# A softmax denominator in cross-attention: three of four probability tiles added up by an accumulating transfer

## The chip, the cores and the metric

The kernel runs on one core of one Trainium2 chip. The metric is the device time of one execution, in microseconds (us). Five engines work in parallel, each through its own queue of instructions in program order: TensorE (PE in the profile; PEld is its weight load), VectorE (DVE), ScalarE (ACT), GpSimd (POOL) and SyncE (SP, which here only issues transfers). They meet through semaphores. Transfers run on the core's 16 DMA engines, whoever issues them. SBUF is the working memory of 128 partitions, PSUM the memory into which matmuls write.

## What is computed

The model is one layer: x (512 tokens of 512) attends to a context of 8192 rows of 384 (cross-attention, then an MLP), then to itself in a window (local attention), then comes a feed-forward block with quantised weights. Only the cross-attention is touched.

```python
def xattn(x, y, Wq, bq, Wk, bk, Wv, bv, W1, b1, W2, b2):     # x: 512 x 512, y: 8192 x 384
    q = (x @ Wq + bq).reshape(B, N, 16, 32)
    k = (y @ Wk + bk).reshape(B, M, 16, 32)
    v = (y @ Wv + bv).reshape(B, M, 16, 32)
    scores = jnp.einsum('bnhd,bmhd->bhnm', q, k) / sqrt(32)
    attn = jax.nn.softmax(scores, axis=-1)                    # over the 8192 keys
    out = jnp.einsum('bhnm,bmhd->bnhd', attn, v).reshape(B, N, 512)
    return jax.nn.relu(out @ W1 + b1) @ W2 + b2
```

The softmax needs, for each head and each of the 512 queries, the sum over all 8192 keys of exp(score). That sum, the denominator, is what the change is about.

## The kernel before

The cross-attention stage walks 16 heads. A head has 16 **quads** of 512 keys (`QUADS`), a quad has four **tiles** of 128 keys (`BT`). The names that matter:

- `scores` (L1079): for a tile, four fp16 matmuls side by side in the PE array write 128 keys x 512 queries to one of three PSUM banks. ACT (L1261) turns it into exp and writes it to `prob[:, q % 4, t]`, in SBUF, float32, 128 x 512. `prob` has four slots (`PSLOTS`), so quad q reuses the slot of quad q - 4.
- `pre` (L1042): the same product turned the other way round, for the head after the next one or so, from which DVE (L1297, `tile_max`) takes each query's maximum. Four tiles per quad. Its PSUM banks are three, too.
- `weighted` (L1092): for each quad, four float32 matmuls with the values, accumulated over the head in one bank.
- The denominator. Of a quad's four probability tiles, GpSimd adds the first `pool_tiles(q)` into `sum_pool` (L1435 and L1439): three tiles at q = 0, 1 and every odd q, two at the other even ones. `add_to_denominator` (L1103) puts the remaining one or two tiles through PE: products with a matrix of ones, which sum over the partitions, accumulated in the bank `den_ps`. Each such tile is four matmuls of 128 x 128, and is done two quads after its exp. At the head's end `denominator` (L1119) sends GpSimd's three summed tiles through the same products; it stands at the end of quad 1 of the next head. DVE then takes the reciprocal (`invert`, L1309) in quad 2, `output` (L1130) folds the weighted sums in quad 5, and DVE scales them (L1316) in quad 6.
- In the last head (15) GpSimd does nothing; DVE adds up two tiles of each quad (`sum_tiles`, L1345 and L1349) and PE takes the rest.

PE's order within a quad is written out by hand: `PE_ORDER = ((0,), 0, (1,), 1, "den", 2, (2,), 3, (3,))`, where `(j,)` is a `pre` tile, a number a `scores` tile and "den" the place of `add_to_denominator`; `weighted` of the quad before follows behind.

Before it writes a slot of `prob`, ACT waits until the slot's last readers are through: `pv_done` (the weighted product of quad q - 4), `den_added` (PE's ones-products of it) and `pool_summed` (GpSimd's add of it). GpSimd's own queue holds nothing but its adds in this stage. SP's queue issues the loads of keys (in four chunks per head, each 256 KB and 128 KB) and of values (1024 KB per head) for the head after the next, and the stores of the outputs.

Of the kernel before, what the change touches and what calls it, by code (L numbers as in the profile page):

```python
# [22 lines left out]
ALU = mybir.AluOpType  # L23
# [15 lines left out]
H = 16  # L39
# [19 lines left out]
POOL_TILES = 3  # L59
# [72 lines left out]
def perceiver(nc, a, out):  # L132

    with ExitStack() as whole:
# [104 lines left out]
        fold_in = sem("fold_in")  # L239
# [45 lines left out]
        with ExitStack() as st:  # L285
# [100 lines left out]
            def _(sp):  # L386
# [9 lines left out]
                sp.dma_start(fold[:], a["c_fold"]).then_inc(fold_in, 16)  # L396
# [453 lines left out]
        with ExitStack() as st:  # L850
# [12 lines left out]
            sum_pool = piece([2, POOL_TILES * T])  # L863
# [17 lines left out]
            pool_summed = sem("pool_summed")  # L881
            pv_read = sem("pv_read")
# [48 lines left out]
            def pool_tiles(q):  # L931

                return POOL_TILES if q < 2 or q % 2 else POOL_TILES - 1


            LAST_SUMMED = QUADS - 2

            def summed_tiles(h, q):

                if not (isinstance(h, int) and h == H - 1):  # L940
                    return pool_tiles(q)
                return DVE_TILES if q < LAST_SUMMED else 0
# [94 lines left out]
            def _(pe):  # L1037
# [58 lines left out]
                def add_to_denominator(i, s, q):  # L1096

                    h = 2 * i + s
                    if q == 0:
                        wait(pe, recip_ready, h)  # L1100
                    for n in range(summed_tiles(h, q), BT):
                        for t in range(TT):
                            last = nc.tensor.matmul(den_ps[t * HD:(t + 1) * HD, 0:P], ones[:],  # L1103
                                                    prob[:, q % PSLOTS, n, t * P:(t + 1) * P],
                                                    start=q == 0 and n == summed_tiles(h, q), stop=False)
                    last.then_inc(den_added, 1)

                def denominator(i, s):

                    h = 2 * i + s  # L1110
                    if isinstance(h, int) and h == H - 1:
                        pe.wait_ge(dve_summed, LAST_SUMMED)
                        tiles = DVE_TILES
                    else:
                        pe.wait_ge(pool_summed, QUADS * (h + 1))
                        tiles = POOL_TILES
                    for n in range(tiles):
                        for t in range(TT):
                            last = nc.tensor.matmul(den_ps[t * HD:(t + 1) * HD, 0:P], ones[:],  # L1119
                                                    sum_pool[:, s, n * T + t * P:n * T + (t + 1) * P],  # L1120
                                                    start=False, stop=n == tiles - 1)
# [17 lines left out]
                def head(i, s, first, last):  # L1139
# [3 lines left out]
                    for q in range(QUADS):  # L1143
                        ahead = last >= (1 if q < QUADS - AHEAD else 2)
                        for step in PE_ORDER:
                            if step == "den":
                                if q >= 2:
                                    add_to_denominator(i, s, q - 2)
                                elif not first:
                                    add_to_denominator(*before, QUADS - 2 + q)  # L1150
# [8 lines left out]
                        if q == 1 and not first:  # L1159
# [10 lines left out]
                pe.wait_ge(fold_in, 16)  # L1170
                pe.wait_ge(ones_row, 16)
# [12 lines left out]
                denominator(LASTPAIR, 1)  # L1184
# [43 lines left out]
            def _(act):  # L1228
# [64 lines left out]
            def _(dve):  # L1293
# [43 lines left out]
                def sum_tiles(q):  # L1337

                    sums = sum_pool[:, 1, 0:DVE_TILES * T].rearrange("p (n t) -> p n t", n=DVE_TILES)
                    if q:  # L1340
                        dve.wait_ge(p_ready, BT * quad_no(LASTPAIR, 1, q) + DVE_TILES)
                    if q == 1:

                        dve.wait_ge(den_ready, H - 2)
                        nc.vector.tensor_tensor(sums, prob[:, 0, 0:DVE_TILES], prob[:, 1, 0:DVE_TILES],  # L1345
                                                ALU.add).then_inc(dve_summed, 2)
                    elif q > 1:
                        dve.wait_ge(dve_summed, q)
                        nc.vector.tensor_tensor(sums, sums, prob[:, q % PSLOTS, 0:DVE_TILES],  # L1349
# [74 lines left out]
            def _(pool):  # L1424

                def add_up(i, s, q):
                    Q = quad_no(i, s, q)
                    n = pool_tiles(q)
# [877 lines left out]
```

## Time and profile before

| what | value |
|---|---|
| median of 3 runs | 1386.98 us |
| lowest and highest | 1385.68 and 1387.59 us |
| the profiled execution: span from first to last instruction | 1383.2 us |
| cross-attention stage, heads 0 to 14 | about 343 to 1079 us of the span |
| one head in that stage | about 48.6 us |

The profile is of one execution. Its span of 1383.2 us is 3.8 us short of the median of the runs; the profiled execution has no other time of its own. A row of a view by stretches gives for each engine the busy time in that stretch with the number of instructions in brackets, then the granted PE clock as a share of the full 2.4 GHz, the mean busy share of the 16 DMA engines, and what they moved.

### The profile page before, as it was taken

The page shows a single profiled execution, that of the slowest core. Times are in us where ns is not written, and L with a number is a line of the kernel's source. Part 1 is how long each engine was busy: PE and PEld are TensorE (multiplying, and loading weights), DVE is VectorE, ACT ScalarE, POOL GpSimd, SP SyncE. Part 2 cuts the span into 40 slices and gives each one's busy share as a digit, 9 for nine tenths or more (in the row PEclk, how much of TensorE's full clock was granted, in tenths as well). Part 3 has the DMA queues.
Part 4 walks back from the last instruction along what each step waited for, and adds up shares of the span by engine and source line. Part 5 has one row for each costly group of instructions (what it writes and reads, how often), then busy time and mean ns, then how long its engine had stood idle before and what let it go on. Part 6 is the DMA issues. An engine that isn't in the chain of part 4 may idle for free. (4 is left out here: it accounts for less than half of the span.)

```text
span 1383.2 us, 39979 instructions
## 1 busy us (share of the span) xinstructions
PE 1332.2 (96%) x17098; PEld 702.8 (51%) x17098; DVE 1120.9 (81%) x1786; ACT 806.1 (58%) x1459; POOL 778.7 (56%) x320
## 2 busy tenths in 40 slices
PE   7999999998999999999999999999999999999898
PEld 4444444443555555555555555545555445566454
DVE  5778888887888888888888888888887746578895
ACT  4454444443777777776777776776777841354332
POOL 0322222122899988988998898899889100201121
PEclk9999999999999999999999999999999999999999
DMA  8568777786352122122212112211210030491000
GB/s 265 177 169 231 207 211 211 210 238 177 91 183 69 39 69 67 30 65 67 69 39 68 56 38 69 67 50 57 59 66 31 5 145 1 92 214 41 0 9 23
DMA packets 127799, 137.54 MB, mean 99 GB/s; under 512 B 44995, under 2 KB 108995, under 8 KB 125699
## 3 DMA queue, kind: packets, MB, share of 16 engines
q1 hardware_dynamic: 127622, 134.98, 34.6%
q8 instruction: 135, 2.21, 0.7%
q14 instruction: 42, 0.34, 0.1%
HBM read 75.70 MB, written 44.17 MB: 87 GB/s over the span
## 5 line engine op out<-in xcount | busy, mean ns | idle before, releaser
L1297 DVE TENSOR_REDUCE early<-attend_banks 128x1 f32<-128x512 f32 x952 | 612.4, 685 | 80.8 <-PE attend_banks L1042 75.6
L1261 ACT ACTIVATE attend_prob<-attend_banks 128x512 f32<-128x512 f32 x1024 | 536.0, 599 | 200.8 <-PE attend_banks L1079 198.6
L1439 POOL TENSOR_TENSOR early<-early,attend_prob 128x1024 f32<-128x1024 f32 x210 | 614.5, 2926 | 37.7 <-ACT attend_prob L1261 9.6
L1079 PE MATMUL attend_banks<-early,k_first 97*32 97x512 f16 x2560 | 258.9, 382 | 3.1 <-ACT attend_prob L1261 3.1
L1042 PE MATMUL attend_banks<-k_first,early 96*32 96x512 f16 x2272 | 235.1, 382 | 1.1 <-PEq L285 1.1
L1079 PE MATMUL attend_banks<-early,attend_k_rest 97*32 97x512 f16 x1536 | 154.1, 381 | 2.8 <-ACT attend_prob L1261 2.8
L1042 PE MATMUL attend_banks<-attend_k_rest,early 96*32 96x512 f16 x1536 | 155.8, 380 | 0.0
L1103 PE MATMUL attend_banks<-attend_prob,ones 128*32 128x128 f32 x3048 | 134.3, 272 | 3.6 <-DVE attend_recip L1309 3.6
L1092 PE MATMUL attend_banks<-attend_prob,wkv_area 128*32 128x512 f32 x1024 | 134.1, 592 | 0.0
L1092 PE MATMUL attend_banks<-attend_prob,attend_vh_odd 128*32 128x512 f32 x1024 | 133.6, 592 | 0.0
L503 POOL TENSOR_TENSOR project_w_whole<-project_grid,project_qscale 128x704 f32<-128x704 f32 x24 | 33.3, 1386 | 173.0 <-DVE project_grid L636 173.0
L1103 PEld LDWEIGHTS attend_banks<-attend_prob,ones 128*32 128x32 f32 x3048 | 95.6, 110 | 54.5 <-DVE attend_recip L1309 11.1
L1079 PEld LDWEIGHTS attend_banks<-early,k_first 97*32 97x32 f16 x2560 | 77.3, 97 | 85.6 <-ACT attend_prob L1261 46.6
L1042 PEld LDWEIGHTS attend_banks<-k_first,early 96*32 96x32 f16 x2272 | 71.3, 97 | 58.4 <-issue 34.9
L555 ACT ACTIVATE project_v<-project_v_ps 128x512 f32<-128x512 f32 x64 | 38.1, 597 | 92.1 <-PE project_v_ps L771 92.1
L497 POOL TENSOR_TENSOR project_qn<-early,project_qinv 128x704 f32<-128x704 f32 x24 | 37.9, 1580 | 87.6 <-issue 50.2
L539 ACT ACTIVATE early<-project_k_ps,project_bk 128x512 f32<-128x512 f32 x64 | 44.0, 688 | 63.6 <-PE project_k_ps L752 61.6
L769 PE MATMUL project_v_ps<-project_w_hi,project_yT_hi 128*128 128x512 f16 x192 | 73.9, 385 | 5.7 <-ACT project_v L555 5.7
L1079 PEld LDWEIGHTS attend_banks<-early,attend_k_rest 97*32 97x32 f16 x1536 | 47.0, 96 | 57.8 <-ACT attend_prob L1261 38.1
L752 PE MATMUL project_k_ps<-project_yT_hi,project_w_hi 128*128 128x512 f16 x192 | 72.5, 379 | 2.3 <-ACT project_q_hi L574 1.4
L770 PE MATMUL project_v_ps<-project_w_lo,project_yT_hi 128*128 128x512 f16 x192 | 73.9, 385 | 0.0
L771 PE MATMUL project_v_ps<-project_w_hi,project_yT_lo 128*128 128x512 f16 x192 | 73.7, 384 | 0.0
(220 smaller groups left out, 1823.6 us busy)
## 6 DMA issues: line engine op xcount, KB each, us to landing
v_scratch<-project_v SPq DMA_DIRECT2D x16, 1024.0 KB, 8.9
early<-in_ctx_dram SPq DMA_DIRECT2D x16, 768.0 KB, 6.2
k_first<-k_scratch SPq DMA_DIRECT2D x36, 256.0 KB, 3.5
k_scratch<-project_k_hi SPq DMA_DIRECT2D x64, 128.0 KB, 2.9
k_scratch<-project_k_lo SPq DMA_DIRECT2D x64, 128.0 KB, 3.1
attend_vh_odd<-v_scratch SPq DMA_DIRECT2D x8, 1024.0 KB, 5.0
wkv_area<-v_scratch SPq DMA_DIRECT2D x7, 1024.0 KB, 4.8
attend_k_rest<-k_scratch SPq DMA_DIRECT2D x24, 256.0 KB, 3.5
```

The lines of the kernel that those rows point to most:

```text
L539: nc.scalar.activation(kf[:, g % 2], k_ps[:, g % 2], ACT.Identity, bias=bk[:, g:g + 1], scale=1.0 / WSCALE).then_inc(kf_ready, 1)
L752: last = nc.tensor.matmul(k_ps[:, g % 2], (w_lo if p == 2 else w_hi)[:, 0, k, cols], (yT_lo if p == 1 else yT_hi)[:, u, k], start=(k, p) = ...
L769: nc.tensor.matmul(v_ps[:, t % 2], yT_hi[:, u, k, cols], w_hi[:, 1, k], start=k == 0, stop=False)
L770: nc.tensor.matmul(v_ps[:, t % 2], yT_hi[:, u, k, cols], w_lo[:, 1, k], start=False, stop=False)
L771: last = nc.tensor.matmul(v_ps[:, t % 2], yT_lo[:, u, k, cols], w_hi[:, 1, k], start=False, stop=k == CK - 1)
L1042: last = nc.tensor.matmul(pre_ps[c * HD:(c + 1) * HD, bank, :], q_stack[0:KROWS, h, queries], keys_at(s, part * BLK, (part + 1) * BLK)[0:K ...
L1079: last = nc.tensor.matmul(s_ps[c * HD:(c + 1) * HD, s_bank[n], :], key_rows[:, c * HD:(c + 1) * HD], q_stack[0:KROWS + 1, h, :], start=Tru ...
L1092: last = nc.tensor.matmul(pv_ps[t * HD:(t + 1) * HD, :], vh[s][:, BT * q + t, :], prob[:, q % PSLOTS, t, :], start=q == 0, stop=q == QUADS ...
L1103: last = nc.tensor.matmul(den_ps[t * HD:(t + 1) * HD, 0:P], ones[:], prob[:, q % PSLOTS, n, t * P:(t + 1) * P], start=q == 0 and n == summ ...
L1261: nc.scalar.activation(prob[:, q % PSLOTS, t, :], s_ps[:, s_bank[BT * q + t]], ACT.Exp, scale=SCALE).then_inc(p_ready, 1)
L1297: nc.vector.tensor_reduce(part_max[:, s, j, part:part + 1], pre_ps[:, bank], AX.X, ALU.max).then_inc(pre_read, 1)
L1439: nc.gpsimd.tensor_tensor(sums, sums, prob[:, q % PSLOTS, 0:n], ALU.add).then_inc(pool_summed, 1)
```

## The change

GpSimd adds only one tile per quad (`POOL_TILES = 1`), the tile 0. The other three (`SENT_TILES`) are one contiguous piece of `prob` in each partition, 128 x 1536 float32 or 768 KB, and go by a transfer that GpSimd issues (`send`) into `sent[:, s, q % 2]`, which lies in SBUF, too. For q = 0 and 1 it is a plain copy, for the 14 others it has `accum_op=add`: the DMA engines read what is in the destination, add what they bring and write it back. There are two destinations, even and odd quads, each with its own semaphore `sent_in`. A send waits for the exps of its quad and for the send before it to the same destination.

PE has no more ones-products inside the heads 0 to 14. `denominator` takes seven tiles (one of GpSimd's, two times three of the transfers') in one block and stands at the end of quad 2 of the next head; `invert` moves from quad 2 to quad 4. ACT's wait before a slot is now for `pv_done`, `pool_summed` and `sent_in` of quad q - 4. In the last head the work is as before, but the products of quads 0 and 1 are made together in quad 3, since the denominator bank is taken until then. `sum_pool` shrinks and gets its own memory; the ones row's and the fold matrix's loads share a semaphore.

```diff
-POOL_TILES = 3
+POOL_TILES = 1
+SENT_TILES = BT - POOL_TILES
...
-            sum_pool = piece([2, POOL_TILES * T])
+            sent = piece([2, 2, SENT_TILES, T])
+            sum_pool = sb("sum_pool", [P, 2, POOL_TILES * T])
+            sum_last = sent[:, 1, 0, 0:DVE_TILES]
...
+            DEN_AT = 2
...
                 def denominator(i, s):
 
                     h = 2 * i + s
...
+                    wait(pe, recip_ready, h)
+                    pe.wait_ge(pool_summed, QUADS * (h + 1))
+                    tiles = [sum_pool[:, s, n * T:(n + 1) * T] for n in range(POOL_TILES)]
+                    tiles += [sent[:, s, u, n] for u in range(2) for n in range(SENT_TILES)]
+                    for n, tile in enumerate(tiles):
+                        if n == POOL_TILES:
+                            pe.wait_ge(sent_in[0], transfers(i, s, QUADS - 2))
+                            pe.wait_ge(sent_in[1], transfers(i, s, QUADS - 1))
+                        for t in range(TT):
+                            last = nc.tensor.matmul(den_ps[t * HD:(t + 1) * HD, 0:P], ones[:],
+                                                    tile[:, t * P:(t + 1) * P],
+                                                    start=n == 0, stop=n == len(tiles) - 1)
                     last.then_inc(den_ready, 1)
...
                             if step == "den":
-                                if q >= 2:
-                                    add_to_denominator(i, s, q - 2)
-                                elif not first:
-                                    add_to_denominator(*before, QUADS - 2 + q)
+                                if last == 0 and q > DEN_AT:
+                                    for behind in range(0 if q == DEN_AT + 1 else q - 2, q - 1):
+                                        add_to_denominator(i, s, behind)
...
-                        if q == 1 and not first:
+                        if q == DEN_AT and not first:
                             denominator(*before)
...
                         wait(act, pv_done, Q + 1 - PSLOTS)
-                        wait(act, den_added, Q + 1 - PSLOTS)
                         if last > 0 or q < PSLOTS:
                             wait(act, pool_summed, Q + 1 - PSLOTS)
+                            wait(act, sent_in[q % 2], transfers(i, s, q - PSLOTS))
                         else:
+                            act.wait_ge(den_added, q + 1 - PSLOTS)
...
-                        if q == 2 and not first:
+                        if q == (DEN_AT + 2 if last > 0 else DEN_AT) and not first:
                             invert(*before)
...
+                def send(i, s, q):
+                    pool.wait_ge(p_ready, BT * (quad_no(i, s, q) + 1))
+                    wait(pool, sent_in[q % 2], transfers(i, s, q - 2))
+                    if q < 2:
+                        wait(pool, den_ready, 2 * i + s - 1)
+                        nc.gpsimd.dma_start(sent[:, s, q % 2], prob[:, q % PSLOTS, POOL_TILES:BT]).then_inc(
+                            sent_in[q % 2], 16)
+                    else:
+                        nc.gpsimd.dma_start(sent[:, s, q % 2], prob[:, q % PSLOTS, POOL_TILES:BT],
+                                            accum_op=ALU.add).then_inc(sent_in[q % 2], 16)
+
+                def head(i, s):
+                    for q in range(QUADS):
+                        add_up(i, s, q)
+                        send(i, s, q)
```

PE's queue around the end of a head, before. L1042 is `pre`, L1079 `scores`, L1092 `weighted`, L1103 and L1119 the ones-products; the block of 12 is at the end of quad 1 of the next head.

```order
L1103 MATMUL attend_banks<-attend_prob,ones 32x128 x4
L1079 MATMUL attend_banks<-early,k_first 32x512 x4
L1042 MATMUL attend_banks<-k_first,early 32x512 x4
L1079 MATMUL attend_banks<-early,k_first 32x512 x4
L1042 MATMUL attend_banks<-k_first,early 32x512 x4
L1092 MATMUL attend_banks<-attend_prob,wkv_area 32x512 x4
L1119 MATMUL attend_banks<-early,ones 32x128 x12
L1042 MATMUL attend_banks<-attend_k_rest,early 32x512 x4
L1079 MATMUL attend_banks<-early,k_first 32x512 x4
L1042 MATMUL attend_banks<-attend_k_rest,early 32x512 x4
L1079 MATMUL attend_banks<-early,k_first 32x512 x4
L1103 MATMUL attend_banks<-attend_prob,ones 32x128 x4
```

The same engine after, at the end of quad 2 of the next head; each function's line is one or eleven higher (1043, 1080, 1093, 1130).

```order
L1080 MATMUL attend_banks<-early,k_first 32x512 x8
L1043 MATMUL attend_banks<-attend_k_rest,early 32x512 x4
L1080 MATMUL attend_banks<-early,k_first 32x512 x4
L1043 MATMUL attend_banks<-attend_k_rest,early 32x512 x4
L1093 MATMUL attend_banks<-attend_prob,wkv_area 32x512 x4
L1130 MATMUL attend_banks<-attend_sum_pool,ones 32x128 x4
L1130 MATMUL attend_banks<-early,ones 32x128 x24
L1043 MATMUL attend_banks<-attend_k_rest,early 32x512 x4
L1080 MATMUL attend_banks<-early,k_first 32x512 x4
L1043 MATMUL attend_banks<-attend_k_rest,early 32x512 x4
L1080 MATMUL attend_banks<-early,k_first 32x512 x8
```

The groups of four ones-products inside the quads are gone, so two `scores` tiles stand next to each other, and one block of 28 stands where 12 stood, a quad later.

GpSimd's queue in head 0 before, from its second quad:

```order
L1439 TENSOR_TENSOR early<-early,attend_prob 128x1024 [waits attend_pool_summed,attend_p_ready]
L1439 TENSOR_TENSOR early<-early,attend_prob 128x1536 [waits attend_pool_summed,attend_p_ready]
L1439 TENSOR_TENSOR early<-early,attend_prob 128x1024 [waits attend_pool_summed,attend_p_ready]
L1439 TENSOR_TENSOR early<-early,attend_prob 128x1536 [waits attend_pool_summed,attend_p_ready]
```

and after (L1455 and L1458 are the sends, copying and accumulating; `early` holds `sent`):

```order
L1455 DMA early<-attend_prob 128x1536 [waits attend_p_ready]
L1443 TENSOR_TENSOR attend_sum_pool<-attend_prob 128x512 [waits attend_p_ready]
L1455 DMA early<-attend_prob 128x1536 [waits attend_p_ready]
L1447 TENSOR_TENSOR attend_sum_pool<-attend_sum_pool,attend_prob 128x512 [waits attend_pool_summed,attend_p_ready]
L1458 DMA early<-attend_prob 128x1536 [waits attend_sent_in0,attend_p_ready]
L1447 TENSOR_TENSOR attend_sum_pool<-attend_sum_pool,attend_prob 128x512 [waits attend_pool_summed,attend_p_ready]
L1458 DMA early<-attend_prob 128x1536 [waits attend_sent_in1,attend_p_ready]
```

One add of two or three tiles per quad has become one add of one tile and one transfer of three, and each transfer waits in GpSimd's queue for the one two quads back.

## Rows read from the trace of the kernel before

**Rows 1.** The page: busy time, share of the span and instructions, by engine.

```profile
PE 1332.2 (96%) x17098; PEld 702.8 (51%) x17098; DVE 1120.9 (81%) x1786; ACT 806.1 (58%) x1459; POOL 778.7 (56%) x320
```

**Rows 2.** Busy time by stretches: start:end, length, engines, clock, DMA share, GB/s.

```profile
343.30:1079.00 735.70, 727.88 (x12908) 387.45 (x12908) 632.31 (x997) 523.02 (x998) 666.57 (x225) 1.00 0.22 64
398.00:446.50 48.50, 48.03 (x864) 25.78 (x858) 42.17 (x67) 34.60 (x66) 44.17 (x16) 1.00 0.46 143
645.00:693.00 48.00, 47.53 (x860) 25.84 (x853) 41.75 (x66) 34.41 (x66) 43.69 (x16) 1.00 0.20 59
336.00:350.00 14.00, 11.27 (x121) 6.33 (x123) 9.54 (x17) 7.02 (x12) 2.33 (x2) 0.88 0.89 261
```

**Rows 3.** Timeline of PE at a head's end: start, length, line, idle before.

```profile
493.56 1.04 PE L1092 MATMUL attend_banks<-attend_prob,attend_vh_odd 128*32 128x512 f32 x8
494.42 0.83 PE L1119 MATMUL attend_banks<-early,ones 128*32 128x128 f32 x24
495.08 0.40 PE L1042 MATMUL attend_banks<-k_first,early 96*32 96x512 f16 x4
495.30 0.40 PE L1079 MATMUL attend_banks<-early,k_first 97*32 97x512 f16 x4
...
496.34 0.43 PE L1103 MATMUL attend_banks<-attend_prob,ones 128*32 128x128 f32 x8 [0.21 <-DVE attend_recip L1309]
```

**Rows 4.** Groups of instructions, whole span: shapes and count, busy us, mean ns, idle.

```profile
L1103 PE MATMUL attend_banks<-attend_prob,ones 128*32 128x128 f32 x3048 | 134.3, 272 | 3.6 <-DVE attend_recip L1309 3.6
L1119 PE MATMUL attend_banks<-early,ones 128*32 128x128 f32 x376 | 13.1, 273 | 0.0
```

**Rows 5.** Waits of the stretch 400 to 1060 us: total us, times, longest.

```profile
ACT attend_prob L1261 <- PE attend_banks L1079: 176.5, 191, 1.4
DVE early L1297 <- PE attend_banks L1042: 66.6, 270, 0.5
PEld attend_banks L1079 <- ACT attend_prob L1261: 61.1, 215, 0.8
```

**Rows 6.** Groups by form, 400 to 1080 us: GpSimd's adds, DVE's work.

```profile
L1439 POOL TENSOR_TENSOR early<-early,attend_prob 128x1536 f32<-128x1536 f32 x98 | 340.5, 3475 | 21.7 <-ACT attend_prob L1261 9.6
L1439 POOL TENSOR_TENSOR early<-early,attend_prob 128x1024 f32<-128x1024 f32 x98 | 232.9, 2377 | 14.0
...
L1309 DVE RECIPROCAL attend_recip<-attend_banks 128x128 f32<-128x128 f32 x14 | 13.4, 957 | 9.0 <-PE attend_banks L1119 9.0
L1316 DVE TENSOR_TENSOR attend_o_out<-attend_banks,attend_recip 128x128 f32<-128x128 f32 x14 | 4.1, 292 | 4.7 <-issue 4.1 <-PE attend_banks L1130 0.6
L1304 DVE TENSOR_REDUCE early<-early 128x4 f16<-128x64 f32 x14 | 3.1, 220 | 0.5
```

**Rows 7.** Timelines: two of DVE's reductions on end, four of ACT's exps.

```profile
355.39 1.29 DVE L1297 TENSOR_REDUCE early<-attend_banks 128x1 f32<-128x512 f32 x2 [0.23 <-PE attend_banks L1042]
...
450.25 2.07 ACT L1261 ACTIVATE attend_prob<-attend_banks 128x512 f32<-128x512 f32 x4 [0.95 <-PE attend_banks L1079]
```

**Rows 8.** Busy time by stretches around a load of values issued at 735.86.

```profile
736.00:737.00 1.00, 1.00 (x30) 0.57 (x20) 0.94 (x2) 1.00 (x3) 0.12 (x1) 1.00 0.21 25
738.00:739.00 1.00, 1.00 (x28) 0.67 (x24) 0.67 (x2) 0.43 (x1) 0.93 (x1) 1.00 0.99 418
739.00:740.00 1.00, 1.00 (x28) 0.45 (x20) 0.64 (x1) 0.14 (x1) 1.00 (x1) 1.00 1.05 442
740.00:741.00 1.00, 0.79 (x20) 0.48 (x20) 1.00 (x3) 0.94 (x2) 1.00 (x1) 1.00 0.07 16
```

**Rows 9.** Transfers by issue: count, KB each, median us from issue to landing; SP's issue times.

```profile
attend_vh_odd<-v_scratch SPq DMA_DIRECT2D x8, 1024.0 KB, 5.0
local_kq_stack<-turned_area SPq DMA_DIRECT2D x24, 128.0 KB, 2.6
...
732.34 0.45 SPq L245 DMA_DIRECT2D attend_k_rest<-k_scratch  x1
732.84 1.82 SPq L246 DMA_DIRECT2D attend_k_rest<-k_scratch  x1
```

More of the change, by code:

```diff
@@ L881, in perceiver @@
             pool_summed = sem("pool_summed")
+            sent_in = [sem(f"sent_in{u}") for u in range(2)]
             pv_read = sem("pv_read")
@@ L929, in keys_at, with summed_tiles, transfers @@
                 return k_rest[:, lo - CHK:hi - CHK]
-            def pool_tiles(q):
-                return POOL_TILES if q < 2 or q % 2 else POOL_TILES - 1
             LAST_SUMMED = QUADS - 2
-            def summed_tiles(h, q):
-                if not (isinstance(h, int) and h == H - 1):
-                    return pool_tiles(q)
+            DEN_AT = 2
+            def summed_tiles(q):
                 return DVE_TILES if q < LAST_SUMMED else 0
+            def transfers(i, s, q):
+                return 16 * (quad_no(i, s, q) // 2 + 1)
             OUT_BANK = S_BANKS + turn_of["output"] % PRE_BANKS
@@ L1096, in add_to_denominator @@
                 def add_to_denominator(i, s, q):
-                    h = 2 * i + s
                     if q == 0:
-                        wait(pe, recip_ready, h)
-                    for n in range(summed_tiles(h, q), BT):
+                        pe.wait_ge(recip_ready, 2 * i + s)
+                    for n in range(summed_tiles(q), BT):
                         for t in range(TT):
@@ L1104, in add_to_denominator, with summed_last @@
                                                     prob[:, q % PSLOTS, n, t * P:(t + 1) * P],
-                                                    start=q == 0 and n == summed_tiles(h, q), stop=False)
+                                                    start=q == 0 and n == summed_tiles(q), stop=False)
                     last.then_inc(den_added, 1)
+                def summed_last():
+                    pe.wait_ge(dve_summed, LAST_SUMMED)
+                    for n in range(DVE_TILES):
+                        for t in range(TT):
+                            last = nc.tensor.matmul(den_ps[t * HD:(t + 1) * HD, 0:P], ones[:],
+                                                    sum_last[:, n, t * P:(t + 1) * P],
+                                                    start=False, stop=n == DVE_TILES - 1)
+                    last.then_inc(den_ready, 1)
                 def denominator(i, s):
                     h = 2 * i + s
[L1111 to L1117, printed above, removed]
+                    wait(pe, recip_ready, h)
[6 more added lines that the diff above has]
+                            pe.wait_ge(sent_in[1], transfers(i, s, QUADS - 1))
                         for t in range(TT):
                             last = nc.tensor.matmul(den_ps[t * HD:(t + 1) * HD, 0:P], ones[:],
-                                                    sum_pool[:, s, n * T + t * P:n * T + (t + 1) * P],
-                                                    start=False, stop=n == tiles - 1)
+                                                    tile[:, t * P:(t + 1) * P],
+                                                    start=n == 0, stop=n == len(tiles) - 1)
                     last.then_inc(den_ready, 1)
@@ L1168, in head @@
                             row(h + 1, 1 - s, n % PRE_BANKS)
-                pe.wait_ge(fold_in, 16)
-                pe.wait_ge(ones_row, 16)
+                pe.wait_ge(ones_row, 32)
                 pe.wait_ge(ones_set, 1)
@@ L1183, in _ @@
                 add_to_denominator(LASTPAIR, 1, QUADS - 1)
-                denominator(LASTPAIR, 1)
+                summed_last()
                 def hidden(m, chunks):
```

26 lines of the change are left out of this document (10 added, 16 removed).

## The prediction

> **What bounds the kernel now.** I read the busy shares first: PE is busy for 96% of the span, DVE 81%, the others under 60% [rows 1]. An average over stages says little of one stage, so the stretches come next. From 343.3 to 1079 us, heads 0 to 14, PE is busy for 727.9 of 735.7 us at the full clock; in one 48 us piece of it PE has 47.53, GpSimd 43.69, DVE 41.75, ACT 34.41, and the DMA engines are busy for a share of 0.20 [rows 2]. So PE sets the pace, 48.6 us per head or 3.04 us per quad. The waits agree: ACT and DVE wait for PE (176.5 and 66.6 us in 660); PE's matmuls wait for hardly anyone, only its weight loads do, ahead of time [rows 5]. DMA has four fifths of its time free, and nobody waits for it. That free time is what the change spends.
>
> **What one step of PE costs.** Busy times of matmuls overlap, so I take starts from the timeline [rows 3]. A group of four `pre` or `scores` matmuls starts 0.22 us before the next. The `weighted` group takes 494.42 - 493.56 = 0.86 us. The block of three ones-tiles takes 495.08 - 494.42 = 0.66, so 0.22 each. A quad without ones-products is 8 x 0.22 + 0.86 = 2.62 us.
>
> **What the change takes off PE.** Before, a head has 26 ones-tiles: 14 quads with one or two (7 x 2 + 7 x 1 = 21), quads 0 and 1 with one each, and 3 at the end. The trace bears it out: each tile leaves 8 records, 3048 / 8 = 381 = 15 x 23 + 36 and 376 / 8 = 47 = 15 x 3 + 2 [rows 4]. After, it has 7. So 19 tiles x 0.22 = 4.18 us per head go, 62.7 us for 15 heads. The stall of PE on the reciprocal, 3.6 us in all [rows 4], goes too, since the bank is next written a head later. Together 66 us. The last head has the same products, four tiles of them in one quad instead of two and two; I set that at nothing, as PE computes the same and waits for one reciprocal as before.
>
> **What hides the rest.** The block of seven tiles (1.54 us) stands behind a `weighted` group: 2.4 us without a new score. ACT has three banks to work through, at 2.07 / 4 = 0.52 us each, so it idles for about 0.9 us; it idles for 0.95 us in every quad now [rows 7], so it catches up. DVE's reductions start 1.29 - 0.69 = 0.60 us apart when nothing is missing (two of them in 1.29 us, of which the last has its 0.69) [rows 7]: 64 x 0.60 + 0.96 + 0.29 + 0.22 = 39.9 us per head [rows 6], under the 44.4 that PE would need. `invert` two quads later is still ahead of `output` in quad 5. GpSimd's add of one tile: two tiles take 2377 ns, three 3475, so one about 2377 - 1098 = 1.28 us [rows 6]. The issue of a transfer by GpSimd is not in the trace; SP's take 0.45 to 1.82 us [rows 9]. That makes 1.7 to 3.1 us per quad. I take the middle, 2.4, hidden under whatever the quad takes.
>
> **What the change adds: the DMA engines.** Fifteen heads send 16 pieces of 128 x 1536 x 4 = 786,432 bytes. First the plain price. In the middle of a load of values the engines are busy for a share of 0.99 and 1.05 and move 418 and 442 GB/s [rows 8]: at a full share 430 GB/s. A plain send is then 1.83 us of all 16 engines. That is the price of the two copies of each head, and the lower bound for an accumulating one; less than a copy it can't be, since it moves all that a copy moves. There is no accumulating transfer in this trace. What it has to do is plain, though: for each byte written two come in, that of the source and that of the destination. If the incoming side is as wide as a copy's, it takes 2 x 1.83 = **3.66 us**. If all three movements take turns, 3 x 1.83 = 5.49, my upper bound. I take 3.66: both reads are unavoidable and 430 GB/s is a busy share of 1.0, so I see no room for the second read; the write can go beside them as in a copy.
>
> The transfers that are there already stay: a share of 0.22 of 735.7 us = 162 us of all engines [rows 2]. The sum for heads 0 to 14:
>
> 15 x (2 x 1.83 + 14 x 3.66) + 162 = 15 x 54.9 + 162 = 985.5 us of DMA time, where the stage had 735.7 us and PE would now want 735.7 - 66 = 669.7.
>
> The engines are then the bound, and the stage is 985.5 - 735.7 = 250 us longer: 1383.2 + 250 = **1633 us** of span, and with the 3.8 us by which the runs' median lies above the span **1637 us**, against 1387.
>
> **Who waits.** A late transfer holds up GpSimd (the send two quads later, and the add queued behind it), and through `sent_in` ACT, which can't write the slot of quad q - 4; then PE has no exps for `weighted` and no free score bank, and the `pre` tiles that DVE wants are queued behind. Nothing is left to cover it; everyone runs at DMA's pace, 64.6 us per head or about 4.1 per quad. The chain of each destination could be tighter still: landing of a 128 KB move within SBUF takes 2.6 us [rows 9], of which 0.3 are data, so an accumulating send about 2.3 + 3.66 + 1 for its issue = 7 us, and there are two chains: 3.5 us per quad, just under DMA's own 3.66. So I add nothing for it.
>
> A rule of the Trainium skill bears on this price. "Collectives: The Full Stack", section "The bandwidth ceiling", holds that a reducing transfer is slower than a copying one not for the addition but for its two source reads on one ring, with a measured ratio of 1.93. As an estimate from that page an accumulating send would be 1.93 x 1.83 = 3.53 us and the result 1609 us. No run here shows it yet.
>
> **The rivals.**
>
> *Rival 1, not slower: the second read is free.* If the engines read faster than they write, an accumulating send costs what a copy does. DMA then needs 15 x 16 x 1.83 + 162 = 601 us, less than PE's 669.7; PE stays the bound and the kernel gains the whole 66: **1321 us**. It decides at a price: up to (669.7 - 162 - 15 x 3.66) / 210 = 2.16 us per send the gain is whole, and at 2.47 us, where the same sum is made with 735.7, it is nil. For it speaks that the 430 GB/s may be set by memory outside SBUF or by the write; against it that both directions would have to be far from equal.
>
> *Rival 2, in between: the price lies between 2.3 and 3.2 us.* At 2.8 us the stage takes 15 x (3.66 + 39.2) + 162 = 805 us, the kernel about **1456 us**. The same place is reached if GpSimd is late: its add and an issue of 1.82 us make 3.1 us per quad, 49.6 per head, 15 us over the 15 heads, **1402 us**; that needs a cheap transfer as well.
>
> *Rival 3, worse: more than a doubled copy.* At 5.49 us the stage takes 15 x (3.66 + 76.9) + 162 = 1370 us and the kernel **2021 us**. Halfway there, another way leads through the clock. PE would be busy for about 670 of 985 us, and in the one stretch of this trace that is as idle, 336 to 350 us with 11.27 of 14 busy, the granted clock is 0.88 [rows 2]. At 1.2 GHz a quad would take 5.5 us of PE, more than DMA's 4.1; if that held half the time, 240 x 0.5 x 1.4 = 168 us come on top: about **1805 us**.
>
> *Rival 4, that it does not do what it says.* The order of instructions shows that the ones-products are gone and 16 sends per head are there, so this has no chance of its own.
>
> **How the numbers follow.** DMA-bound at a price near 3.66 (3.3 to 4.3 us, 1560 to 1770 us): 0.63. Rival 1: 0.15. Rival 2: 0.12. Rival 3: 0.10. The predicted time is that of the first, 1637. The range runs from 1400 to 1850: it leaves out rival 1 (0.15) and about half of rival 3 (0.05). A change of 0.2% (3 us) is about what a measurement here can tell from none. Faster: rival 1 and a sliver of rival 2, 0.16. Same: the narrow window around a price of 2.47 us, 0.02. Slower: the rest, 0.82.
>
> **What the profile after would show.** In the same heads: DMA share near 1.0 where 0.20 stood; PE busy 65 to 70% of the stretch, ACT waiting for a DMA and no longer for PE; 64 to 65 us per head; sends landing 6 to 9 us after their issue; GpSimd busy for a third. I am wrong if the DMA share stays below 0.9 while the head takes over 48.6 us (then the chain, the issue or the add sets the pace, not the engines' capacity), or if heads take 44 us with PE at 99% (rival 1). If PE's granted clock is below 1.00 there, part of the loss is the clock's.

## The result, and the profile after

The changed kernel takes 1702.5 us (median of 4 runs, 1699.9 to 1703.6) against 1386.6 us before: a ratio of 1.2275, with a 95% interval of 1.2258 to 1.2293. It is slower by 316 us. The forecast was 1637 us, with a range of 1400 to 1850. The profiled execution has a span of 1701.8 us, 318.6 us more than the profiled one before.

The page's busy times, to be set beside [rows 1]:

```profile
PE 1387.4 (82%) x14818; PEld 616.3 (36%) x14818; DVE 1116.3 (66%) x1786; ACT 804.5 (47%) x1459; POOL 608.3 (36%) x560
q0 software_dynamic: 34560, 188.76, 53.3%
q1 hardware_dynamic: 127622, 134.98, 27.9%
```

PE has 2280 records fewer, which is the ones-products (285 tiles of 8). The second and third line are from the list of DMA queues: packets, MB, and the time of their packets as a share of 16 engines' span. q0 is new; it holds the sends, 240 x 786,432 bytes = 188.7 MB.

The stage by stretches, columns as in [rows 2] (start:end, length, PE, PEld, DVE, ACT, POOL, granted clock, DMA share, GB/s):

```profile
343.30:1400.00 1056.70, 786.05 (x10696) 302.59 (x10700) 630.74 (x1000) 524.35 (x1005) 496.86 (x465) 0.90 1.00 223
650.00:700.00 50.00, 36.07 (x512) 13.14 (x507) 32.06 (x53) 26.51 (x51) 25.05 (x23) 0.97 1.04 211
```

The DMA share, 0.20 to 0.22 before, is 1.00 over a thousand microseconds. No compute engine is over 75% busy. Who waits for whom has turned round against [rows 5] (total us, times, longest; here over the whole span):

```profile
PEld attend_banks L1080 <- ACT attend_prob L1271: 434.3, 422, 5.5
DVE early L1307 <- PE attend_banks L1043: 398.0, 377, 6.6
POOL early L1458 <- DMA early<-attend_prob: 369.3, 171, 5.2
ACT attend_prob L1271 <- DMA early<-attend_prob: 356.5, 148, 6.3
PE attend_banks L1080 <- ACT attend_prob L1271: 260.8, 163, 5.0
```

This is the chain of the forecast: a send waits for the send two quads back, ACT for its slot, PE for the exps, DVE for PE. The sends themselves, in GpSimd's timeline (start, length, line, idle before):

```profile
742.66 0.89 POOL L1458 DMA_DIRECT2D early<-attend_prob  x1 [1.53 <-DMA early<-attend_prob]
746.39 0.89 POOL L1458 DMA_DIRECT2D early<-attend_prob  x1 [1.55 <-DMA early<-attend_prob]
751.12 0.89 POOL L1458 DMA_DIRECT2D early<-attend_prob  x1 [2.52 <-DMA early<-attend_prob]
755.31 0.89 POOL L1458 DMA_DIRECT2D early<-attend_prob  x1 [1.99 <-DMA early<-attend_prob]
759.00 0.89 POOL L1458 DMA_DIRECT2D early<-attend_prob  x1 [1.50 <-DMA early<-attend_prob]
762.74 0.89 POOL L1458 DMA_DIRECT2D early<-attend_prob  x1 [1.54 <-DMA early<-attend_prob]
```

Three of the five distances are 3.69 to 3.74 us. The two behind the load of keys issued at 744.50 are 4.73 and 4.19. The stretch of the shortest one, with no load issued in it:

```profile
755.31:759.00 3.69, 3.01 (x44) 1.23 (x44) 2.15 (x4) 2.65 (x6) 2.19 (x2) 1.00 1.04 211
```

The engines are full, and one send of 768 KB goes through in that time. So an accumulating send costs the 16 engines about 3.7 us when it has them to itself. A head takes 69.6 us, from the first reciprocal to the one 13 heads later:

```profile
431.87 0.95 DVE L1319 RECIPROCAL attend_recip<-attend_banks 128x128 f32<-128x128 f32 x1
...
1336.31 0.95 DVE L1319 RECIPROCAL attend_recip<-attend_banks 128x128 f32<-128x128 f32 x1
```

Landing has become slow for everyone. Against the 5.0 us of [rows 9] a load of values takes 10.9:

```profile
early<-attend_prob POOLq DMA_DIRECT2D x240, 768.0 KB, 7.9
attend_vh_odd<-v_scratch SPq DMA_DIRECT2D x8, 1024.0 KB, 10.9
```

The changed kernel was run again beside the experiments:

> The changed kernel again, beside the others on the same chip: 1702 us.

It gave 1703.3 us, a ratio of 1.2286 (1.2261 to 1.2310). Ratios in this document are against the kernel before, run beside each experiment (1385.7 to 1386.6 us), with the 95% interval in brackets.

### The profile page after: what moved, and what is told of

It is laid out like the page before. It is cut to its first block and busy times, and to the rows that moved or that the text cites. A ratio compares the mean times of both kernels' runs of the same rounds, so it can differ in the third digit from the quotient of the medians.

```text
span 1701.8 us, 35926 instructions
## 1 busy us (share of the span) xinstructions
PE 1387.4 (82%) x14818; PEld 616.3 (36%) x14818; DVE 1116.3 (66%) x1786; ACT 804.5 (47%) x1459; POOL 608.3 (36%) x560
## 3 DMA queue, kind: packets, MB, share of 16 engines
q1 hardware_dynamic: 127622, 134.98, 27.9%
## 5 line engine op out<-in xcount | busy, mean ns | idle before, releaser
L1080 PE MATMUL attend_banks<-early,k_first 97*32 97x512 f16 x2560 | 241.3, 406 | 179.0 <-ACT attend_prob L1271 179.0
L1458 POOL DMA_DIRECT2D early<-attend_prob x210 | 186.0, 886 | 410.9 <-DMA early<-attend_prob 369.3
L1447 POOL TENSOR_TENSOR attend_sum_pool<-attend_sum_pool,attend_prob 128x512 f32<-128x512 f32 x210 | 324.9, 1547 | 4.0 <-ACT attend_prob L1271 3.1
L1043 PE MATMUL attend_banks<-k_first,early 96*32 96x512 f16 x2272 | 246.9, 411 | 1.1 <-PEq L285 1.1
L1080 PE MATMUL attend_banks<-early,attend_k_rest 97*32 97x512 f16 x1536 | 143.9, 405 | 81.8 <-ACT attend_prob L1271 81.8
L1043 PE MATMUL attend_banks<-attend_k_rest,early 96*32 96x512 f16 x1536 | 160.2, 405 | 0.0
L1093 PE MATMUL attend_banks<-attend_prob,attend_vh_odd 128*32 128x512 f32 x1024 | 148.7, 659 | 0.0
L1093 PE MATMUL attend_banks<-attend_prob,wkv_area 128*32 128x512 f32 x1024 | 148.3, 658 | 0.0
L752 PE MATMUL project_k_ps<-project_yT_lo,project_w_hi 128*128 128x512 f16 x192 | 72.4, 379 | 0.2 <-DVE project_yT_lo L599 0.2
L752 PE MATMUL project_k_ps<-project_yT_hi,project_w_lo 128*128 128x512 f16 x192 | 72.4, 379 | 0.0
## 6 DMA issues: line engine op xcount, KB each, us to landing
attend_vh_odd<-v_scratch SPq DMA_DIRECT2D x8, 1024.0 KB, 10.9
```

The costliest lines, as they stand in the source:

```text
L752: last = nc.tensor.matmul(k_ps[:, g % 2], (w_lo if p == 2 else w_hi)[:, 0, k, cols], (yT_lo if p == 1 else yT_hi)[:, u, k], start=(k, p) = ...
L1043: last = nc.tensor.matmul(pre_ps[c * HD:(c + 1) * HD, bank, :], q_stack[0:KROWS, h, queries], keys_at(s, part * BLK, (part + 1) * BLK)[0:K ...
L1080: last = nc.tensor.matmul(s_ps[c * HD:(c + 1) * HD, s_bank[n], :], key_rows[:, c * HD:(c + 1) * HD], q_stack[0:KROWS + 1, h, :], start=Tru ...
L1093: last = nc.tensor.matmul(pv_ps[t * HD:(t + 1) * HD, :], vh[s][:, BT * q + t, :], prob[:, q % PSLOTS, t, :], start=q == 0, stop=q == QUADS ...
L1447: nc.gpsimd.tensor_tensor(sums, sums, prob[:, q % PSLOTS, 0:POOL_TILES], ALU.add).then_inc(pool_summed, 1)
L1458: nc.gpsimd.dma_start(sent[:, s, q % 2], prob[:, q % PSLOTS, POOL_TILES:BT], accum_op=ALU.add).then_inc(sent_in[q % 2], 16)
```

## Experiments

**The addition left out (copy3).** The question was whether the second read makes the price, or anything sent by GpSimd is slow.

```diff
-                        nc.gpsimd.dma_start(sent[:, s, q % 2], prob[:, q % PSLOTS, POOL_TILES:BT],
-                                            accum_op=ALU.add).then_inc(sent_in[q % 2], 16)
+                        nc.gpsimd.dma_start(sent[:, s, q % 2], prob[:, q % PSLOTS, POOL_TILES:BT]).then_inc(sent_in[q % 2], 16)
```

> The changed kernel with all 16 sends of a head as plain copies; the sums of the sent tiles are left out, so the denominators are those of two quads only. In the changed kernel, where no load is under way, the sends follow each other every 3.73 us. Theory A (the accumulating send reads source and destination, twice the incoming bytes, and the 16 DMA engines are full): a copy costs 1.83 us, heads 0 to 14 need 15 x 16 x 1.83 + 162 = 601 us of DMA, less than PE's 670, so PE is the bound again: about 1321 us, 44.4 us per head, DMA share about 0.9. Rival B (a transfer issued by GpSimd is slow whatever it does, by its descriptors or its issue): no change, about 1690 us. Rival C (the chain: a send waits for the landing two quads back): a landing falls by 1.9 us to about 6, so 3.0 us per quad, about 1390 us.

Measured: 1435.4 us, ratio 1.0356 (1.0326 to 1.0387). Taking the addition out gives back 267 of 317 us. That settles most of it against rival B. But 1321 did not come either. The queue's row, the stretch 500 to 1000 us and three waits in it:

```profile
q0 software_dynamic: 34560, 188.76, 35.2%
500.00:1000.00 500.00, 454.10 (x6825) 187.32 (x6817) 395.15 (x643) 329.59 (x634) 272.37 (x300) 0.97 0.84 297
ACT attend_prob L1271 <- DMA early<-attend_prob: 36.4, 16, 7.8
PE attend_banks L1130 <- DMA early<-attend_prob: 25.2, 10, 3.8
PE attend_banks L1080 <- ACT attend_prob L1271: 20.5, 30, 2.6
```

35.2% of 1432.5 us over 240 copies is 2.10 us each. With 2.10 the forecast's sum for DMA is 15 x 16 x 2.10 + 162 = 666 us, level with the 670 that it gave PE, and the stage takes some 785 us (735.7 and the 49.3 by which the span is longer). The row agrees that the engines are not full on average (0.84). Yet PE is idle for a tenth of the time. The timelines of PE, GpSimd and SP at one head's end show how:

```profile
505.84 0.57 POOL L1458 DMA_DIRECT2D early<-attend_prob  x1 [0.16 <-issue]
506.16 0.34 SPq L965 DMA_DIRECT2D wkv_area<-v_scratch  x1
509.58 0.53 POOL L1455 DMA_DIRECT2D early<-attend_prob  x1 [3.17 <-ACT attend_prob L1271]
511.31 0.39 PE L1130 MATMUL attend_banks<-attend_sum_pool,ones 128*32 128x128 f32 x8
514.96 2.39 PE L1130 MATMUL attend_banks<-early,ones 128*32 128x128 f32 x48 [3.25 <-DMA early<-attend_prob]
```

The head's last send leaves at 505.84, the load of values (1024 KB) at 506.16, and the next send at 509.58. The engines carry all three at once, and PE's block of ones-products stands idle for 3.25 us, until the last sends have landed. The DMA share of this stretch, near 1 for nine microseconds:

```profile
506.00:515.00 9.00, 5.75 (x96) 2.17 (x91) 5.12 (x9) 4.65 (x10) 2.23 (x3) 1.00 0.97 370
```

An average share of 0.84 hides moments in which it is near 1.0 and somebody waits.

**The block moved back (copy3_den3).** If PE's wait at the block were the cost, moving it would bring it back. The edit comes on top of copy3's; the last head keeps its block where it was.

```diff
-            DEN_AT = 2
+            DEN_AT = 3
```

> The run with plain copies (1435 us) with the block of seven ones-tiles one quad later, at the end of quad 3 (quad 2 of the last head), and the reciprocal at quad 5; sums of the sent tiles left out as there. That run's PE waits at the block for the last sends of the head before, 25.2 us in 500 (10 heads). If this wait is what a late landing costs PE, about 2.5 us per head go: 1435 - 38 = about 1397 us. If the sends only meet the next wait (ACT's, for its slot), it stays at 1425 to 1435 us.

Measured: 1437.2 us, ratio 1.0372 (1.0351 to 1.0393), no gain. The waits of the stretch 500 to 1000 us:

```profile
ACT attend_prob L1271 <- DMA early<-attend_prob: 59.4, 33, 4.3
POOL early L1458 <- DMA early<-attend_prob: 101.3, 54, 4.1
PE attend_banks L1080 <- ACT attend_prob L1271: 42.8, 48, 3.6
```

PE's wait at the block is gone from the longest ones, ACT's wait for its slot has grown from 36.4 to 59.4 us, and PE's for ACT from 20.5 to 42.8, nearly what the block had given back. So the block was only the first to meet the late landings. The expectation that 38 us would come back was wrong. That they are late because of the loads beside them is my reading of the timeline above; no run moved a load or gave `prob` more slots.

**No sends (nosend).** What PE's part of the change is worth by itself. The block takes GpSimd's one sum seven times in place of the sent tiles.

```diff
-                        if n == POOL_TILES:
-                            pe.wait_ge(sent_in[0], transfers(i, s, QUADS - 2))
-                            pe.wait_ge(sent_in[1], transfers(i, s, QUADS - 1))
...
-                            wait(act, sent_in[q % 2], transfers(i, s, q - PSLOTS))
...
-                        send(i, s, q)
```

> The changed kernel without any send and without the waits on them; the block of seven ones-tiles stays, and takes GpSimd's one sum seven times, so tiles 1 to 3 of each quad are left out of the denominator. It measures what PE's part of the change is worth alone. Forecast of the blind sum: 66 us less than before, 1321 us; 44.4 us per head. If DVE or ACT or the block of seven sets the pace instead, it stays over 1335 us.

Measured: 1342.4 us, ratio 0.9686 (0.9658 to 0.9714): 43 us less than before, not 66. A head takes 45.8 us (reciprocals at 447.08 and 492.87). PE's timeline has the reason:

```profile
587.72 0.61 PE L1080 MATMUL attend_banks<-early,attend_k_rest 97*32 97x512 f16 x8
588.16 0.39 PE L1043 MATMUL attend_banks<-k_first,early 96*32 96x512 f16 x4
588.46 0.40 PE L1080 MATMUL attend_banks<-early,attend_k_rest 97*32 97x512 f16 x4
588.68 0.39 PE L1043 MATMUL attend_banks<-k_first,early 96*32 96x512 f16 x4
588.90 1.03 PE L1093 MATMUL attend_banks<-attend_prob,attend_vh_odd 128*32 128x512 f32 x8
```

Without the ones-products two `scores` tiles stand next to each other (the x8). PE is then ahead of ACT by a tile, and the fourth `scores` starts 0.30 instead of 0.22 us after the group before it, in this quad and in those around it. If it is so in all, 16 x 0.08 = 1.3 us per head is 19 us in 15 heads. The next run tests this.

**PE's order made alternating (nosend_alt, before_alt).**

```diff
-PE_ORDER = ((0,), 0, (1,), 1, "den", 2, (2,), 3, (3,))
+PE_ORDER = ((0,), 0, (1,), 1, "den", (2,), 2, (3,), 3)
```

> The run without sends (1342 us, where the blind sum had 1321), with PE's order within a quad changed so that pre and scores tiles alternate throughout (0 before, with two scores tiles next to each other where the ones-products stood). Tiles 1 to 3 are left out of the denominator as there. If the missing 21 us is PE waiting for ACT at the second of two adjacent scores tiles (0.08 us per quad, 1.3 us per head, seen in that run's timeline): about 1322 us. If it is something else, 1342 us.

Measured: 1327.1 us, ratio 0.9578 (0.9559 to 0.9597). 15 of the missing 21 us are back, by the order alone. A head takes 44.6 us (reciprocals at 444.57 and 489.19).

> The kernel before with PE's order within a quad changed alone: (2,), 2, (3,), 3 behind the ones-products in place of 2, (2,), 3, (3,). There the ones-products already keep the scores tiles apart, so no change is expected: 1386 us, within 3 us.

Measured: 1382.8 us, ratio 0.9977 (0.9967 to 0.9986). The same line gives the kernel before 3.7 us, a little over what I expected. A head takes 48.5 us instead of 48.8, each measured from the first reciprocal to the one 12 heads later (the 48.6 in the table of the kernel before is 0.2 too low). With the order the same in both, taking the ones-products off PE is worth 1382.8 - 1327.1 = 56 us.

**What the price of a send depends on (acc1, acc2, half16).** First fewer tiles to a send (the arguments of both kinds of send):

```diff
-sent[:, s, q % 2], prob[:, q % PSLOTS, POOL_TILES:BT]
+sent[:, s, q % 2, 0:1], prob[:, q % PSLOTS, POOL_TILES:POOL_TILES + 1]
```

> The changed kernel with only one tile per send (128 x 512, 256 KB); two of the three sent tiles are left out of the denominator, and the block of seven is filled up with GpSimd's sum. Theory A: 3.73 / 3 = 1.24 us per accumulating send, DMA far under PE's pace, about 1321 us. If a send has a large fixed cost on the engines (rows of 2 KB cost as much as rows of 6 KB): about 1690 us.

> The same with two tiles per send (128 x 1024, 512 KB); one tile is left out. Theory A: 2.49 us per accumulating send, 15 x (2 x 1.22 + 14 x 2.49) + 162 = 722 us of DMA against 670 of PE: about 1373 us, with the loads getting in the way up to 1400 us; DMA share near 1.0. With a fixed cost per send, 1450 to 1690 us.

Measured: 1350.0 us, ratio 0.9737 (0.9709 to 0.9766), with one tile; 1497.5 us, ratio 1.0801 (1.0772 to 1.0830), with two. Then half the bytes at the same number of rows and elements, all of them zeros:

```diff
-sent[:, s, q % 2], prob[:, q % PSLOTS, POOL_TILES:BT]
+sent16[:, s, q % 2], zeros16[:]
```

> The changed kernel with sends of 1536 16-bit elements per partition, of zeros, in place of 1536 32-bit ones: as many sends, rows and elements, half the bytes; the sent tiles are left out of the denominator. Theory A (bytes): an accumulating send costs 1.87 us, DMA needs about 15 x (2 x 0.92 + 14 x 1.87) + 162 = 582 us, PE is the bound: 1321 us. Rival D (the addition sets the rate, by elements): unchanged price of 3.73 us, about 1690 us.

Measured: 1393.3 us, ratio 1.0062 (1.0039 to 1.0085). The queue's rows of the three, in this order:

```profile
q0 software_dynamic: 32640, 62.93, 24.2%
q0 software_dynamic: 34560, 125.84, 41.6%
q0 software_dynamic: 32640, 94.39, 34.1%
```

From each I take 30 copies, at 0.70 us per 256 KB (a third of the 2.10 of copy3; that they scale is an assumption), and divide by 210:

| run | bytes per send | share x span, us | price of an accumulating send, us |
|---|---|---|---|
| acc1 | 256 KB | 0.242 x 1350.9 = 326.9 | 1.46 |
| half16 | 384 KB | 0.341 x 1391.3 = 474.4 | 2.11 |
| acc2 | 512 KB | 0.416 x 1493.0 = 621.1 | 2.76 |
| changed kernel | 768 KB | 0.533 x 1701.8 = 907.1 | 4.02 |

The price goes up by 1.3 us for each 256 KB, with some 0.2 us fixed. half16 has the rows and elements of the changed kernel, and its price is that of its bytes. So an addition priced by elements is out (rival D), and so is a cost per row. Per byte written an accumulating send takes 4.02 / 2.10 = 1.91 times as long as a copy. That the reads are what doubles is the reading that fits all four, but an addition priced by bytes would fit them as well: the trace does not show reads by themselves, and no run keeps the second read and leaves out the addition.

The times disagree with the sums in the same way as copy3's, and the expectations were missed by 29 us (acc1), about 100 (acc2) and 72 (half16). With the prices of the table the DMA sum of half16 is 637 us, under PE's 670, and it takes 51 us more than nosend; that of acc2 is 784 us, which would make 1434, and it takes 1497. acc1, with a landing of 4.1 us, is 8 us over nosend. acc2 shows the same waits as copy3, in 500 us of its stage:

```profile
PE attend_banks L1131 <- DMA early<-attend_prob: 32.5, 9, 4.9
ACT attend_prob L1272 <- DMA early<-attend_prob: 61.1, 25, 8.4
```

**A third destination (three).** Is the chain of two the bound, or the engines' capacity? The edit is shown in part; a head has three copies here, its block ten tiles, and `sum_pool` lies in other memory.

```diff
+            sent_2 = sb("sent_2", [P, 2, SENT_TILES, T])
...
-                    wait(pool, sent_in[q % 2], transfers(i, s, q - 2))
+                    wait(pool, sent_in[q % 3], transfers(i, s, last_of(q)))
```

> The changed kernel with three destinations instead of two, so that a send waits for the landing three quads back; a head has 3 copies and 13 accumulating sends, and the block has 10 tiles. Theory A (capacity): only the copy in place of an accumulating send counts, 15 x 1.9 = 28 us less than the 1702 of the changed kernel, about 1674 us, DMA share 1.0 still, and each landing takes longer by a half (about 12 us). Rival C (the chain): a landing of 8 us over three chains is 2.7 us per quad, under PE's pace: about 1330 us.

Measured: 1651.9 us, ratio 1.1919 (1.1884 to 1.1953): 51 us less than the changed kernel, where a copy in place of an accumulating send explains 15 x (4.02 - 2.10) = 29. The DMA share stays at 0.99 and the landing grows to 11.1 us:

```profile
500.00:1000.00 500.00, 372.90 (x5528) 153.10 (x5520) 319.94 (x512) 261.40 (x503) 247.50 (x237) 0.96 0.99 233
early<-attend_prob POOLq DMA_DIRECT2D x165, 768.0 KB, 11.1
q0 software_dynamic: 34560, 188.76, 51.4%
```

Had the chain been the bound, some 370 us would have gone, as the expectation says. The engines are the bound. The 22 us beyond can hardly be engines that idled less, since the share was 1.00 before. By the queue's row the packets were cheaper: 0.514 x 1650.8 = 848.5 us, less 45 copies at 2.10, is 3.87 us for each of 195 accumulating sends, against 4.02. Why they were is open.

**A complete kernel that sends less (mixed, mixed2).** It is built on the kernel before; the edit is shown in part. GpSimd adds three tiles at odd quads and one at even ones, where a send takes three; PE keeps one tile of the odd quads.

```diff
-                return POOL_TILES if q < 2 or q % 2 else POOL_TILES - 1
+                return POOL_TILES if q < 2 or q % 2 else 1
...
+            def is_sent(q):
+
+                return q >= 2 and q % 2 == 0
...
+                    if is_sent(q) and not (isinstance(h, int) and h == H - 1):
+                        return
```

> A complete kernel, built on the kernel before: GpSimd adds three tiles at q = 0, 1 and odd q, and one at the even q from 2 to 14, where the other three go by a send; PE keeps the fourth tile of q = 0, 1 and odd q. A head has 2 copies and 5 accumulating sends, and PE 18 ones-tiles instead of 26. DMA: 15 x (2 x 1.83 + 5 x 3.73) + 162 = 497 us, far from full. GpSimd: 3.47 + 8 x 3.48 - 3.48 + 7 x (1.28 + 0.89) = 43 us per head. PE: 46.3 us per head. So PE stays the bound and 8 x 0.22 x 15 = 26 us go: about 1360 us. If the price of a send does not shrink when the DMA engines are not full, or GpSimd's two extra seconds of waiting show, it is over 1387 us.

Measured: 1382.7 us, ratio 0.9976 (0.9967 to 0.9986). Not 1360. In the second version the block of nine ones-tiles stands a quad later, and PE's order alternates.

> The complete mixed kernel (1383 us) with the block of nine ones-tiles at the end of quad 2 in place of quad 1, and the alternating order. In the mixed kernel's trace a head takes 48.0 us where PE's sum is 46.3; ACT waits 12 us in 500 for a send and PE's block is behind. If the block's wait for late sends and the adjacent scores tiles are what is missing, 46.5 us per head: about 1360 us. If GpSimd (busy 436 of 500 us) is the bound through the wait for its sums, it stays at 1375 to 1383 us.

Measured: 1380.7 us, ratio 0.9962 (0.9949 to 0.9975), the fastest complete kernel here, and of its 5.8 us before_alt's one line has 3.7. Its stage and a wait, 500 to 1000 us:

```profile
500.00:1000.00 500.00, 491.19 (x8323) 240.96 (x8326) 429.80 (x704) 361.80 (x692) 439.20 (x230) 1.00 0.72 174
ACT attend_prob L1296 <- DMA early<-attend_prob: 25.6, 21, 2.2
```

A head takes 47.7 us, where PE's sum is 46.3. The same sum for the kernel before, with eight tiles more at 0.22 us, is 48.1, where it takes 48.8; so half of the 1.4 us between is no matter of the sends. ACT waits for sends 1.2 us per occasion, although the DMA engines are used at 0.72. I had expected the block's place and the order to be the cause; both together brought 2 us. What holds the rest, ACT's waits for sends or GpSimd at 88%, is open. Nor does all that the heads gain arrive: 15 x (48.8 - 47.7) would be 16 us. Between the reciprocals of heads 0 and 1 lie 51.1 us in place of 48.8, and behind the last reciprocal the kernel takes 271.0 us in place of 267.4; I did not look into either.

## Why the prediction was right, and where its steps were off

**The bound.** Right. PE set the pace before, and the 16 DMA engines set it after, with a share of 1.00 and every compute engine idle for a quarter of the stage or more. Of the signs named ahead, the share and the landing (7.9 us) came as said. PE was busy for 74%, not 65 to 70, and ACT still waited 158 us in the stage for PE. A head took 69.6 us, not 64 to 65, where 64.6 was also a slip: 985.5 / 15 is 65.7.

**The price of an accumulating send.** The step that carried the forecast, 2 x 1.83 = 3.66 us, held for sends that follow each other undisturbed (3.69 to 3.74 us). Over the whole stage it is 4.02 by the queue's row, and a copy is 2.10 in place of 1.83. Put into the forecast's sum, 15 x (2 x 2.10 + 14 x 4.02) + 162 = 1069 us against 985.5. That is 84 us more, which would make 1721 us; 1702 was measured. The mis-sized term is thus the rate of the sends: I took it from the middle of one undisturbed load [rows 8], where the stage mixes sends with loads of keys and values. The rate itself holds for copies. In copy3, in a stretch in which only q0 had packets, they move 430 GB/s at a share of 1.04:

```profile
551.00:552.00 1.00, 1.00 (x25) 0.49 (x17) 0.66 (x2) 0.59 (x1) 0.00 (x0) 1.00 1.04 430
```

Part of the difference lies in the count: the share goes above 1 when the engines are full (1.04 in the stretch of 3.69 us, which makes 3.84 us by this count), so a price from the queue's row is higher than the time that a send takes. The rest, 3.84 to 4.02, came beside loads, and it is the sends' packets alone that took longer. The loads' term of the sum held, as the queue's row before shows,

```profile
q1 hardware_dynamic: 127622, 134.98, 34.6%
```

34.6% of 1383.2 us being 479 us and 27.9% of 1701.8 us 475.

**The rule of the Trainium skill.** "Collectives: The Full Stack", section "The bandwidth ceiling", gives 1.93 for a reducing against a copying transfer, measured between two collectives. The runs here give 4.02 / 2.10 = 1.91 within SBUF. Its cause, two reads, fits the test by bytes, which does not prove it. The estimate of 1609 us made with it was low because the copy's price was.

**PE's saving.** The number of products was right, the gain was not: 43 us instead of 66. What stood between two `scores` tiles went, and ACT could not follow. With the tiles alternating (nosend_alt) a head took 4.2 us less than before, which is the forecast's 19 x 0.22, and the kernel 59 us less. The step "what hides the rest" looked at ACT's share and at the one long block, and not at the order inside a quad. In the changed kernel this cost nothing, being hidden by DMA.

**Waiting at the ends.** I added nothing for the chain and nothing for waits on landings. In the saturated kernel that holds to within some 20 us, the 19 by which the sum above is too high. It is where rival 1 fails: I had it that a send at 2.16 us or less gives the whole gain and at 2.47 breaks even. copy3 has 2.10 us per send and loses 50 us. The sum of capacities is a lower bound of the time, and I used it as the time. Had an accumulating send cost no more than a copy, the change would still have been slower than before. The forecast never needed this step, since its own case was the full one; with a cheap send it would have been 114 us off.

**The clock.** In the stage it is 0.90 of full speed, where it was 1.00, with stretches of 4 us at 0.5 to 0.7 after PE's pauses. I take this to cost nothing here, since PE then still waits for ACT for 261 us; no run tested it, and rival 3's second way did not come about.

**GpSimd.** An accumulating issue takes 0.89 us, a copying one 0.57, inside the bounds of 0.45 and 1.82. One tile's add takes 1.28 us, as worked out. Issue and add together take 2.2 us of the 4.4 that a quad lasts, so GpSimd was busy for half the time rather than a third (47%), and waited 369 us for sends; it was not the bound in the changed kernel.

## What to carry to other kernels

Price a transfer that accumulates at twice a copy of the same bytes, and count it against the DMA engines' time as one counts work on any engine; "four fifths free" was 38 us per head, and the change asked for 60. When the sum of an engine's work comes near the time there is, the sum is only the floor. What counts then, as I read copy3, is the slowest landing beside a large load, against the number of slots that wait for it; that last part is argued, not tested. Before work is taken out of a tuned order, look at what it kept apart.

## What was not expected of the hardware

- A copy of 768 KB within SBUF, issued by GpSimd, occupies the engines for 2.10 us on average in a stage with loads, against 1.83 by the rate of an undisturbed load. With copies and no load under way the rate was that of the load, 430 GB/s.
- An accumulating send of 16-bit elements costs about half of one of as many 32-bit elements (2.11 against 4.02 us), and lies on the line of the 32-bit ones by bytes (1.46 us for 256 KB, 2.76 for 512).
- GpSimd begins its add before the accumulating issue ahead of it has ended. The issue takes 0.89 us, a copying one 0.57. The add behind it is recorded with 1.58 us instead of 1.28, but starts 0.61 us after the issue's start, and from the issue's end to its own it takes 1.30 us: it is no slower, the two records overlap by 0.28 us. From the start of the issue to the end of the add it is 2.19 us in the changed kernel (the first pair) and 1.88 with a copying issue in copy3 (the second):

```profile
742.66 0.89 POOL L1458 DMA_DIRECT2D early<-attend_prob  x1 [1.53 <-DMA early<-attend_prob]
743.27 1.58 POOL L1447 TENSOR_TENSOR attend_sum_pool<-attend_sum_pool,attend_prob 128x512 f32<-128x512 f32 x1
...
503.80 0.57 POOL L1458 DMA_DIRECT2D early<-attend_prob  x1 [1.94 <-DMA early<-attend_prob]
504.38 1.30 POOL L1447 TENSOR_TENSOR attend_sum_pool<-attend_sum_pool,attend_prob 128x512 f32<-128x512 f32 x1
```
